# A second of every four chunks gets its right neighbour on VectorE instead of TensorE

## The chip, the cores and the metric

The kernel runs on one core of a Trainium2 chip. The metric is the device time of one execution in microseconds (us); lower is better. "DVE" in the rows is VectorE, "PE" TensorE ("PEld" its weight loads), "ACT" ScalarE, "POOL" GpSimd, "SP" the sync engine, which only issues transfers.

## What is computed

The input x is 8 images of 128 channels, 256 x 256, float32. Two layers, each of the form x + f(groupnorm(x)), follow each other. The first is the one that matters here:

```python
# each channel is shifted by its own sub-pixel amount (|theta| <= 1), so each point is a
# blend of four neighbours; then scaled per channel, then a 1x1 convolution over channels
s = z1*(1-dy)*(1-dx) + z2*(1-dy)*dx + z3*dy*(1-dx) + z4*dy*dx
s = s * w_dw[None, :, None, None]
return jnp.einsum('bchw,oc->bohw', s, w_pw)
...
x = x + _L0_conv_ref(_gn(x), L0_conv_theta_s, L0_conv_w_dw, L0_conv_w_pw)
x = x + _L1_conv_ref(_gn(x), L1_conv_w_c1, ...)
```

The second layer begins with a Haar transform and a 1x1 convolution (w_c1) on it, followed by a batch norm over all images; the rest (depthwise 3x3, two 1x1 convolutions, the way back) comes after all of that in time and isn't touched.

## The kernel before

**Three parts in time.** The first part (to about 2800 us) computes layer 0 and the first convolution of layer 1 (c1) of all images; it ends where the batch norm needs its totals. The second part (to about 3850 us) does the depthwise and 1x1 convolutions; the third writes the output. The change lies in the first part.

**Chunks, groups, images.** An image is 32 chunks of 8 rows (2048 points per channel). Four chunks are a group (`s` = 0 to 3 is the chunk's place, `SLOTS` = 4), 8 groups (`g`, `NG` = 8) are an image (`b`). Chunk number t = b * 32 + g * 4 + s. The loop over groups in the middle of an image, and the one over images 2 to 5, are hardware loops; the first and last group of an image are written out, since they carry extra work.

**What a chunk costs each engine**, in the order in which its queue has it:

- VectorE (`shift_rows`, L1311): wait for the chunk and the one below it to be in the ring; wait until TensorE has done with the buffers of two chunks ago (`conv_done`, L1322); L1333 adds the upper neighbour to the rows, giving u; two of three pieces of statistics (`count_x`, L1229) of a chunk of the next image; L1349 adds the lower neighbour to u and reports `u_done`; the third piece of statistics; L1359 adds the left neighbour, giving v. Where `three_in_v(b, s)` holds, the third piece comes behind L1359, and L1365 then adds the right neighbour to v as well, after a wait for L1359 through the counter `v_left`. `v_done` is reported by the last of them. u and v each have two buffers, for even and odd chunks.
- TensorE (`conv`, L927): four PSUM banks hold x already. Per half chunk, two matmuls of 128 x 512 float32 with `w_right` on u shifted by one column (L936; they apply the right neighbour), unless `three_in_v`; then two with `w_center` on v (L941). Then `c1`, four matmuls (L963) on a chunk of the image before. In the trace each such matmul appears as two records, so four matmuls are "x8".
- ScalarE (`shift_group`, L712): copies x into PSUM for the next chunk (`put_x`, L605), takes the result as x1 (L642), stores it (L649), squares it (L659), sums a quarter of a chunk of the next image (L673, L676), turns c1's result into y1 (L688, stored at L700) and squares it (L709).
- SP's queue (`load_image`, L377), in program order per chunk: `load_ring` loads x of a later chunk into its ring slot (L357) once `x_in_psum` and the `u_done` of a chunk three places back (four at s = 3) have been reported; `load_x1` (L375) loads a chunk of x1 of the image before back for c1, except the six that are held in SBUF; `load_x_ahead` (L346) loads a chunk of the next image for the statistics, after the counts (`x_counted`, `x_summed`) of the chunk that had the buffer. A wait in this queue holds up everything behind it.
- GpSimd copies single ring rows (L521) at the ends of a group.

The last group of an image has the moments and scales of the next image on VectorE besides (L1246 to L1275), groups 0 and 1 the padding, new weights and moments of x1 (L1239, L1278, L1292), and c1's weights (L1304, L1308) at the end of group 0. Image 7 has no next image, so no statistics; image 0 has no c1 beside it.

`three_in_v` (L314) is true for one place in four, s = 3, in images 1 to 6, for two, s = 1 and 3, in image 7 (`final(b)`), and for none in image 0.

Of the kernel before, what the change touches and what calls it, by code (L numbers as in the profile page):

```python
# [12 lines left out]
B, H, W = 8, 256, 256  # L13
# [6 lines left out]
SLOTS = 4  # L20
NG = NCH // SLOTS
# [26 lines left out]
def preact_kernel(nc, x, theta_s, w_dw, w_pwT, w_c1T, b_c1, bn1_g, bn1_b, dw_w, dw_b, gn_g, gn_b,  # L48
# [5 lines left out]
    with ExitStack() as ctx:  # L54
# [3 lines left out]
        def sem(name):  # L58
            return ctx.enter_context(nc.semaphore(name))
# [185 lines left out]
        def norm_step(s):  # L245

            return (s - NT - 2) // NT if s >= NT + 2 and (s - 2) % NT == 0 and s < TILES + NT else None
# [6 lines left out]
        def slot(s):  # L254
            return ring[:, 1 + s * ROWS:1 + (s + 1) * ROWS, :]
# [19 lines left out]
        u_up, v_done, v_left = sem("u_up"), sem("v_done"), sem("v_left")  # L275
# [25 lines left out]
        def nth(t, back=0):  # L301

            return t + (1 + LEAD - back)
# [9 lines left out]

        def three_in_v(b, s):  # L314

            return not (isinstance(b, int) and b == 0) and (s % 2 == 1 if final(b) else s == SLOTS - 1)

        def final(b):

            return isinstance(b, int) and b == B - 1  # L320
# [834 lines left out]
        def _(dve):  # L1155
# [9 lines left out]
            def done(ins):  # L1165

                steps[1] += 1
                ins.then_inc(dve_step, 1)
                dve.wait_ge(dve_step, steps[0] + steps[1])
# [51 lines left out]
            def count_x(b, g, s, pieces=range(DVE_PIECES)):  # L1221

                chunk, arrived, count = first_chunk(g, s) if isinstance(b, int) and b == 0 else \
                    (ahead[s], ahead_in[s], ahead_count(b, g))
                if 0 in pieces:
                    dve.wait_ge(arrived, count)
                i = g * SLOTS + s
                for r in pieces:
                    last = nc.vector.bn_stats(stats_x[:, bass.ds(i * (6 * DVE_PIECES) + 6 * r, 6)],  # L1229
                                              chunk[:, r * BANK:(r + 1) * BANK])  # L1230
                if DVE_PIECES - 1 in pieces:
                    last.then_inc(x_counted, 1)

            def pad_row(row):
                return ts(ring[:, row, :], ones[:, 0:1].broadcast_to([P, W]), pad_x, None, ALU.mult)

            def pad_columns(k):
                for col in (0, W + 1):
                    last = ts(u_buf[k][:, :, col], ones[:, 0:ROWS], pad_u, None, ALU.mult)  # L1239
                return last  # L1240
# [14 lines left out]
            def group_variance(n, gm, ps_means):  # L1255

                dve.wait_ge(gmom_ready, n)
                done(nc.vector.tensor_copy(gm, ps_means[:, 0:2]))
                done(stt(out=tmp, in0=gm[:, 0:1], scalar=gm[:, 0:1], in1=gm[:, 1:2],
                         op0=ALU.mult, op1=ALU.subtract))  # L1260
                done(ts(tmp, tmp, 0.0, -1.0, ALU.min, ALU.mult))
                ts(var, tmp, EPS, None, ALU.add).then_inc(var_ready, 1)
# [14 lines left out]
            def x_weights():  # L1277
                ts(w_center[:, :], pwT[:, :], scale0, None, ALU.mult)  # L1278
                ts(w_right[:, :], pwT[:, :], scale0r, None, ALU.mult).then_inc(shift_ready, 1)

            def x_bias(n):
                dve.wait_ge(vec_done, n)
                ts(bias0, ps_small_x[:, 4:5], -1.0, None, ALU.mult).then_inc(bias0_ready, 1)

            def keep_first(b):
                dve.wait_ge(sq_done, nth(b * NCH + (SLOTS - 1)))
                done(nc.vector.tensor_copy(sums_x1[:, :, 0:SLOTS], sums_first[:, :, :]))

            def x1_moments(b):
                dve.wait_ge(x1_ready, nth((b * NCH + (NCH - 1)) * 2 + 1))  # L1290
                dve.wait_ge(sq_done, nth(b * NCH + (NCH - 1)))
                nc.vector.tensor_reduce(mom[:, 0:1], sums_x1[:, 0:2, :].rearrange("p a n -> p (a n)"),  # L1292
                                        mybir.AxisListType.X, ALU.add)
                done(nc.vector.tensor_reduce(mom[:, 1:2], sums_x1[:, 2, :], mybir.AxisListType.X, ALU.add))
                ts(mom, mom, 1.0 / (H * W), None, ALU.mult).then_inc(mom_ready, 1)

            def x1_scales(n):
                group_root(n)
                tt(q1, rstd, gmom[:, 0:1], ALU.mult).then_inc(vec_ready, 1)
# [11 lines left out]
            def shift_rows(b, g, s, before, tail, ahead_of, place):  # L1311

                t = b * NCH + g * SLOTS + s
                k = s % 2
                first, last = place == "first", place == "last"
                nx, n1 = b * 2 + 2, b * 2 + 1
                for near in range(s, min(s + 2, SLOTS)):
                    dve.wait_ge(slot_in[near], b * (16 * NG) + g * 16 + 16)
                if s == 0 and not first:
                    dve.wait_ge(top_copied, b * (NG - 1) + g)  # L1320

                dve.wait_ge(conv_done, nth(t * 2 + 1, 4))  # L1322
                if first and s == 0:
                    pad_columns(0)
                    done(pad_row(0))
                if first and s == 1:
                    done(pad_columns(1))
                    if not (isinstance(b, int) and b == 0):
                        x_weights()
                if last and s == 0:  # L1330
                    done(pad_row(SLOTS * ROWS + 1))
                u = u_buf[k][:, :, 1:W + 1]
                stt(out=u, in0=ring[:, s * ROWS:(s + 1) * ROWS, :], scalar=up, in1=slot(s),  # L1333
                    op0=ALU.mult, op1=ALU.add).then_inc(u_up, 1)
                late = last and s == 0
                if first and s == 1:

                    dve.wait_ge(x1_ready, nth(b * (2 * NCH), 1))
                    x_bias(1 if isinstance(b, int) and b == 0 else b * 2)
                if first and s == 2 and before:  # L1340
                    group_variance(n1, gmom, ps_small)
                if last and s == 2 and not final(b):
                    group_variance(nx, gmom_x, ps_small_x)
                if ahead_of and not late:
                    count_x(*ahead_of, s, range(0, 2))
                dve.wait_ge(u_up, t + 1)
                if s == SLOTS - 1 and not last:
                    dve.wait_ge(bottom_copied, b * (NG - 1) + (g + 1))
                stt(out=u, in0=ring[:, s * ROWS + 2:(s + 1) * ROWS + 2, :], scalar=down, in1=u,  # L1349
                    op0=ALU.mult, op1=ALU.add).then_inc(u_done, 1)  # L1350
                if first and s == 1 and before:
                    x1_moments(b - 1)
                if late:
                    keep_first(b)
                if ahead_of and not late and not three_in_v(b, s):
                    count_x(*ahead_of, s, range(2, DVE_PIECES))
                dve.wait_ge(u_done, nth(t))
                v = v_buf[k].rearrange("p (r c) -> p r c", c=W)
                left_added = stt(out=v, in0=u_buf[k][:, :, 0:W], scalar=left, in1=u, op0=ALU.mult, op1=ALU.add)  # L1359
                if three_in_v(b, s):  # L1360
                    left_added.then_inc(v_left, 1)
                    if ahead_of and not late:
                        count_x(*ahead_of, s, range(2, DVE_PIECES))
                    dve.wait_ge(v_left, g * 2 + ((B - 2) * NG + s // 2 + 1) if final(b) else b * NG + (g + (1 - NG)))
                    stt(out=v, in0=u_buf[k][:, :, 2:W + 2], scalar=right, in1=v,  # L1365
                        op0=ALU.mult, op1=ALU.add).then_inc(v_done, 1)
                else:
                    left_added.then_inc(v_done, 1)
                if late and not final(b):
                    x_moments(b + 1, nx)  # L1370
                if ahead_of and late:
                    count_x(*ahead_of, s)
                if last and s == 2 and not final(b):
                    x_scales(nx)
                if first and s == 2 and before:
                    x1_scales(n1)
                if first and s == 3 and before:
                    c1_weights(b - 1, n1)
# [130 lines left out]
            for s in range(TILES + OLD_LAG + 2):  # L1509
                q = s - OLD_LAG  # L1510
                b = norm_step(s)
# [124 lines left out]
```

## Time and profile before

| | us |
|---|---|
| median of 3 runs | 5349.4 (5344.71 to 5351.09) |
| the profiled execution, its own time | 5349.64 |
| span in the profile | 5348.0 |
| TensorE busy | 4636.7 (87%) |
| VectorE busy | 4607.9 (86%) |
| ScalarE busy | 4341.1 (81%) |
| GpSimd busy | 1152.0 (22%) |

Rows of the trace give times from the span's start. In windows, "(x84)" is a count of instructions, PEclk the granted TensorE clock as a share of 2.4 GHz (0.5 is its lower level, 1.2 GHz), the DMA share the mean busy share of the 16 DMA engines, and GB/s what they moved. A window is attributed by start time for DMA packets. In the timeline, instructions of one line that follow each other are merged, with their count at the end.

### The profile page before, as it was taken

The numbers are of one execution on the slowest core, as the hardware profiler recorded it, in microseconds if no ns is written. First come the engines' busy times: TensorE is split into PE (matmuls) and PEld (weight loads), VectorE is DVE, ScalarE is ACT, GpSimd is POOL, SyncE is SP. The second block draws the span as 40 slices with busy tenths as digits, with TensorE's granted clock in tenths as the row PEclk, the third lists the DMA queues.
The fourth block names the chain that finished last, engine by engine and source line by source line (L and its number), as shares of the span: only waits on it lengthen the run. The fifth ranks groups of instructions, "written<-read, shape, count | busy, mean of one in ns | idle before, by whom it ended". The sixth has DMA issues, their size and how long they took to land. (4 is left out here: it accounts for less than half of the span.)

```text
span 5348.0 us, 54815 instructions
## 1 busy us (share of the span) xinstructions
PE 4636.7 (87%) x12574; PEld 2144.3 (40%) x12574; DVE 4607.9 (86%) x4207; ACT 4341.1 (81%) x6467; POOL 1152.0 (22%) x855
## 2 busy tenths in 40 slices
PE   2789999999999999999998999999987777777775
PEld 1233334344343443444443666666642222222222
DVE  7999899898998989999907999999568888888887
ACT  5788888888888888888846888888578888888887
POOL 0000000000000000000005888888301111111111
PEclk7999999999999999999999999999999999999998
DMA  8999999999999999998972333333159999999999
GB/s 337 346 351 362 426 404 414 425 383 425 394 414 425 381 425 400 416 405 332 381 283 95 134 134 135 136 136 135 51 113 225 236 236 236 236 235 236 235 236 224
DMA packets 248866, 1542.05 MB, mean 288 GB/s; under 512 B 29424, under 2 KB 29808, under 8 KB 91504
## 3 DMA queue, kind: packets, MB, share of 16 engines
q1 hardware_dynamic: 156528, 936.14, 44.9%
q0 software_dynamic: 36864, 268.45, 24.2%
q10 hardware_dynamic: 55296, 335.57, 15.0%
q8 instruction: 53, 0.87, 0.1%
q14 instruction: 125, 1.02, 0.1%
HBM read 877.35 MB, written 662.70 MB: 288 GB/s over the span
## 5 line engine op out<-in xcount | busy, mean ns | idle before, releaser
L1142 PE MATMUL ps<-arena,c2T 128*128 128x512 f32 x2048 | 1024.3, 651 | 366.8 <-ACT arena L891 364.5
L963 PE MATMUL ps<-arena 128*128 128x512 f32 x2048 | 980.8, 623 | 40.2 <-DMA arena<-out_x 23.3
L941 PE MATMUL ps<-arena 128*128 128x512 f32 x2048 | 966.0, 598 | 45.1 <-DVE arena L1365 22.4
L936 PE MATMUL ps<-arena 128*128 128x512 f32 x1536 | 740.7, 605 | 79.7 <-DVE arena L1349 35.2
L1142 PEld LDWEIGHTS ps<-arena,c2T 128*128 128x128 f32 x2048 | 401.4, 205 | 989.0 <-ACT arena L891 559.7
L891 ACT ACTIVATE arena<-ps,small 128x512 f32<-128x512 f32 x1024 | 713.7, 778 | 98.6 <-DVE arena L1574 90.1
L1333 DVE SCALAR_TENSOR_TENSOR arena<-arena,shift 128x2048 f32<-128x2048 f32 x256 | 601.8, 2351 | 162.0 <-DMA arena<-in_x 100.9
L1458 DVE SCALAR_TENSOR_TENSOR ps<-arena,taps,ps 128x256 f32<-128x256 f32 (+1 forms) x604 | 655.8, 1133 | 19.6 <-PE ps L1087 19.0
L605 ACT ACTIVATE ps<-arena 128x1024 f32<-128x1024 f32 x512 | 526.4, 1028 | 159.8 <-ACT arena L642 146.9
L521 POOL TENSOR_SCALAR arena<-arena 128x256 f32<-128x256 f32 x112 | 103.9, 936 | 2518.8 <-DMA arena<-in_x 2387.3
L642 ACT ACTIVATE arena<-ps,small 128x1024 f32<-128x1024 f32 x512 | 565.0, 1104 | 91.1 <-PE ps L941 89.3
L963 PEld LDWEIGHTS ps<-arena 128*128 128x128 f32 x2048 | 388.8, 192 | 577.7 <-issue 568.8
L941 PEld LDWEIGHTS ps<-arena 128*128 128x128 f32 x2048 | 386.6, 191 | 566.2 <-issue 469.2
L1359 DVE SCALAR_TENSOR_TENSOR arena<-arena,shift 128x2048 f32<-128x2048 f32 x256 | 599.1, 2340 | 3.5
L1349 DVE SCALAR_TENSOR_TENSOR arena<-arena,shift 128x2048 f32<-128x2048 f32 x256 | 598.6, 2338 | 1.9
L898 ACT ACTIVATE arena<-arena 128x2048 f32<-128x2048 f32 x256 | 490.4, 1916 | 113.5 <-DVE arena L1582 110.7
L1229 DVE BATCH_NORM_STATS2 arena<-arena 128x512 f32 (+1 forms) x768 | 497.2, 681 | 20.9 <-DMA arena<-in_x 20.9
L578 POOL DMA_DIRECT2D out_x<-arena x256 | 218.1, 852 | 1320.2 <-ACT arena L898 1287.2
L1581 DVE TENSOR_TENSOR arena<-arena 128x1024 f32<-128x1024 f32 x256 | 314.3, 1228 | 209.5 <-DMA out_x<-arena 208.5
L659 ACT ACTIVATE arena<-arena 128x2048 bf16<-128x2048 f32 x256 | 484.8, 1894 | 0.5 <-ACT arena L642 0.5
L936 PEld LDWEIGHTS ps<-arena 128*128 128x128 f32 x1536 | 287.1, 191 | 476.6 <-issue 350.0
L564 POOL TENSOR_TENSOR arena<-arena 128x1024 f32<-128x1024 f32 x128 | 302.9, 2367 | 99.6 <-ACT arena L840 54.5
(169 smaller groups left out, 5907.7 us busy)
## 6 DMA issues: line engine op xcount, KB each, us to landing
arena<-in_x SPq DMA_DIRECT2D x508, 1024.0 KB, 14.4
out_x<-arena ACTq DMA_DIRECT2D x256, 1024.0 KB, 9.0
out_x<-arena POOLq DMA_DIRECT2D x256, 1024.0 KB, 17.0
arena<-out_x SPq DMA_DIRECT2D x208, 1024.0 KB, 16.7
y_dram<-arena ACTq DMA_DIRECT2D x128, 512.0 KB, 8.5
arena<-y_dram SPq DMA_DIRECT2D x128, 512.0 KB, 3.6
h_dram<-arena SPq DMA_DIRECT2D x112, 512.0 KB, 2.7
arena<-h_dram SPq DMA_DIRECT2D x112, 512.0 KB, 10.2
```

The lines of the kernel that those rows point to most:

```text
L605: nc.scalar.activation(banks(half), ring[:, bass.ds(1 + s * ROWS + half * 4, 4), :] .rearrange("p r c -> p (r c)"), ACT.Copy).then_inc(x_i ...
L642: nc.scalar.activation(x1_made(s, place)[:, half * (CH // 2):(half + 1) * (CH // 2)], banks(half), ACT.Identity, bias=bias0, accum_out=tot ...
L891: last = nc.scalar.activation(g_buf[k][:, q, :], ps[:, 4 * k + q, :], ACT.Gelu, bias=z_bias[:, q:q + 1], scale=z_scale[:, q:q + 1])
L936: mm(ps[:, r, :], w_right[:, :], u_buf[k][:, 2 * r:2 * r + 2, 2:W + 2], start=False, stop=False, skip_group_check=True)
L941: last = mm(ps[:, r, :], w_center[:, :], v_buf[k][:, r * BANK:(r + 1) * BANK], start=False, stop=True, skip_group_check=True)
L963: last = mm(ps[:, 4 + s % 2, :], w_c1b[:, q, :], cells[:, q // 2, q % 2, :, :], start=(q == 0), stop=(q == 3))
L1142: last = mm(ps[:, 4 * k + q, :], c2T[:, q, :], h2[:, k * HC:(k + 1) * HC], start=True, stop=True)
L1229: last = nc.vector.bn_stats(stats_x[:, bass.ds(i * (6 * DVE_PIECES) + 6 * r, 6)], chunk[:, r * BANK:(r + 1) * BANK])
L1333: stt(out=u, in0=ring[:, s * ROWS:(s + 1) * ROWS, :], scalar=up, in1=slot(s), op0=ALU.mult, op1=ALU.add).then_inc(u_up, 1)
L1349: stt(out=u, in0=ring[:, s * ROWS + 2:(s + 1) * ROWS + 2, :], scalar=down, in1=u, op0=ALU.mult, op1=ALU.add).then_inc(u_done, 1)
L1359: left_added = stt(out=v, in0=u_buf[k][:, :, 0:W], scalar=left, in1=u, op0=ALU.mult, op1=ALU.add)
L1458: stt(out=acc, in0=h_tile(t, dy, dx, first), scalar=tap_weight(dy, dx), in1=acc, op0=ALU.mult, op1=ALU.add).then_inc(dw_acc, 1)
```

## The change

The second neighbour-in-v chunk of each group, until now only in image 7, is there in images 1 to 6 as well. In those chunks TensorE's four matmuls L936 are left out, VectorE executes L1365, and its third piece of statistics comes behind L1359 rather than before it. The value awaited on `v_left` is renumbered, since there are now two such chunks in every group from image 1 on.

```diff
@@ -313,7 +313,7 @@
         def three_in_v(b, s):
 
-            return not (isinstance(b, int) and b == 0) and (s % 2 == 1 if final(b) else s == SLOTS - 1)
+            return not (isinstance(b, int) and b == 0) and s % 2 == 1
 
@@ -1361,7 +1361,7 @@
                     left_added.then_inc(v_left, 1)
                     if ahead_of and not late:
                         count_x(*ahead_of, s, range(2, DVE_PIECES))
-                    dve.wait_ge(v_left, g * 2 + ((B - 2) * NG + s // 2 + 1) if final(b) else b * NG + (g + (1 - NG)))
+                    dve.wait_ge(v_left, b * (2 * NG) + g * 2 + (s // 2 + 1 - 2 * NG))
                     stt(out=v, in0=u_buf[k][:, :, 2:W + 2], scalar=right, in1=v,
                         op0=ALU.mult, op1=ALU.add).then_inc(v_done, 1)
```

## Rows read from the trace of the kernel before

**Rows 1.** The page, part 2: GB/s moved in 40 slices of 133.7 us.

```profile
GB/s 337 346 351 362 426 404 414 425 383 425 394 414 425 381 425 400 416 405 332 381 283 95 134 134 135 136 136 135 51 113 225 236 236 236 236 235 236 235 236 224
```

**Rows 2.** Windows, images 4 and 7: stretch, its us, busy us (count) of each engine, clock, DMA.

```profile
core 0: us, PE busy (x) PEld busy (x) DVE busy (x) ACT busy (x) POOL busy (x), PEclk, DMA share, GB/s
...
1399.70:1733.50 333.80, 317.71 (x713) 134.25 (x712) 304.38 (x246) 282.47 (x515) 12.41 (x14) 0.98 0.99 409
...
2390.00:2662.90 272.90, 270.36 (x617) 116.47 (x617) 256.47 (x131) 232.00 (x371) 21.23 (x14) 0.99 0.93 362
```

**Rows 3.** Windows, groups 0 to 7 of image 4, same columns.

```profile
1399.70:1439.90 40.20, 36.97 (x84) 15.70 (x82) 39.82 (x45) 30.84 (x57) 2.27 (x2) 0.96 0.99 402
1439.90:1481.10 41.20, 40.82 (x90) 17.68 (x91) 36.89 (x27) 33.98 (x63) 1.66 (x2) 0.96 0.84 316
1481.10:1519.50 38.40, 38.40 (x89) 16.62 (x88) 36.67 (x26) 34.01 (x64) 2.64 (x2) 1.00 1.01 425
1519.50:1559.20 39.70, 38.99 (x89) 16.46 (x88) 36.82 (x26) 34.13 (x63) 2.76 (x2) 1.00 1.01 426
1559.20:1601.60 42.40, 40.72 (x92) 16.95 (x91) 36.99 (x26) 36.84 (x69) 0.81 (x2) 1.00 1.01 424
1601.60:1644.80 43.20, 41.72 (x95) 17.50 (x94) 36.88 (x25) 37.00 (x68) 0.81 (x2) 1.00 1.01 426
1644.80:1688.80 44.00, 41.23 (x93) 16.82 (x93) 37.30 (x27) 39.02 (x70) 1.46 (x2) 1.00 1.01 425
1688.80:1733.50 44.70, 38.86 (x88) 16.52 (x87) 43.01 (x50) 36.65 (x70) 0.00 (x0) 0.96 1.01 424
```

**Rows 4.** Timeline, VectorE, image 4: start, us, instruction, [idle before <- what ended it].

```profile
1449.23 2.35 DVE L1333 SCALAR_TENSOR_TENSOR arena<-arena,shift 128x2048 f32<-128x2048 f32 x1 [0.65 <-PE ps L941]
...
1470.16 2.35 DVE L1333 SCALAR_TENSOR_TENSOR arena<-arena,shift 128x2048 f32<-128x2048 f32 x1 [1.82 <-PE ps L941]
...
1481.12 2.35 DVE L1333 SCALAR_TENSOR_TENSOR arena<-arena,shift 128x2048 f32<-128x2048 f32 x1
...
1666.44 2.35 DVE L1333 SCALAR_TENSOR_TENSOR arena<-arena,shift 128x2048 f32<-128x2048 f32 x1 [2.52 <-DMA arena<-in_x]
...
1675.01 2.35 DVE L1333 SCALAR_TENSOR_TENSOR arena<-arena,shift 128x2048 f32<-128x2048 f32 x1
```

**Rows 5.** Timeline, TensorE, group 1 and the start of group 2 of image 4.

```profile
1440.28 5.47 PE L963 MATMUL ps<-arena 128*128 128x512 f32 x8 [2.41 <-DVE small L1308]
...
1469.96 3.76 PE L963 MATMUL ps<-arena 128*128 128x512 f32 x8
...
1480.43 3.76 PE L963 MATMUL ps<-arena 128*128 128x512 f32 x8
...
1487.46 3.76 PE L963 MATMUL ps<-arena 128*128 128x512 f32 x8
```

**Rows 6.** Waits, groups 3 to 5 of image 4: total us, times, longest.

```profile
DVE arena L1333 <- DMA arena<-in_x: 9.3, 5, 2.6
```

**Rows 7.** Windows, the boundary stretches of images 1 to 7, columns as in rows 2.

```profile
401.20:482.20 81.00, 70.50 (x154) 30.25 (x153) 76.62 (x70) 61.99 (x107) 2.64 (x4) 0.94 0.88 326
688.80:812.90 124.10, 115.50 (x262) 49.59 (x261) 119.64 (x120) 101.49 (x186) 3.62 (x4) 0.97 0.97 390
1020.30:1147.20 126.90, 116.70 (x260) 49.66 (x260) 119.70 (x119) 101.58 (x187) 3.95 (x4) 0.96 0.95 380
1354.90:1481.10 126.20, 116.65 (x261) 49.91 (x260) 119.79 (x119) 101.52 (x188) 3.92 (x4) 0.96 0.95 381
1688.70:1815.90 127.20, 115.30 (x261) 49.24 (x260) 119.96 (x120) 101.82 (x188) 4.17 (x4) 0.97 0.95 378
2023.30:2147.60 124.30, 114.63 (x260) 49.21 (x259) 119.74 (x119) 102.59 (x188) 5.76 (x4) 0.97 0.97 392
2352.90:2390.00 37.10, 37.10 (x89) 16.34 (x89) 36.30 (x38) 29.04 (x51) 0.00 (x0) 1.00 0.94 364
```

**Rows 8.** DMA issues, groups 6 and 7, then group 1, of image 4: median us to landing.

```profile
arena<-in_x SPq DMA_DIRECT2D x17, 1024.0 KB, 20.2
...
arena<-in_x SPq DMA_DIRECT2D x8, 1024.0 KB, 6.0
```

## The prediction

> **What bounds the kernel now.** The change touches images 1 to 6 of the first part, so I first asked where that part is and what runs in it. The slices of the page show the DMA engines moving 425 GB/s in slice after slice up to about 2400 us, with dips to some 380 [rows 1]. Windows over whole images (from the first L1333 of one to the first of the next) give 333.8 us for image 4, of which TensorE is busy for 317.7, VectorE for 304.4, ScalarE for 282.5, and the DMA share is 0.99 [rows 2]. So four things are nearly full, and an average doesn't say which of them sets the pace. Windows by group of four chunks do [rows 3]. Groups 2 to 7 run at 424 to 426 GB/s, the same figure to within half a per cent while their lengths range from 38.4 to 44.7 us: a ceiling of the transfers, not a pace set elsewhere. Group 0 moves only 402 GB/s and group 1 only 316: there compute sets the pace. The time to landing agrees: a load of 1 MB lands 20.2 us after its issue in the stretch from group 6 on and 6.0 us in group 1 [rows 8]; loads queue in the one and not in the other.
>
> What sets groups 0 and 1 differs. In group 0 VectorE is busy 39.8 of 40.2 us and TensorE 37.0. In group 1 TensorE is busy 40.8 of 41.2 us and VectorE 36.9 [rows 3]: VectorE waits for it before L1333, 0.65 and 1.82 us in the rows shown [rows 4]. The last group is short of both: 44.7 us, VectorE busy for 43.0 (it has the moments and scales of the next image besides), DMA still at 424 GB/s [rows 3].
>
> **VectorE's added work.** A chunk with two neighbours takes 8.57 us from L1333 to L1333 (1666.44 to 1675.01), a chunk with the third addition, L1365, 10.96 (1470.16 to 1481.12) [rows 4]: 2.39 us more. The change makes s = 1 such a chunk in all 8 groups of 6 images: 48 x 2.39 = 115 us of VectorE work. A group goes from 36.8 to 39.2 us in the middle of an image.
>
> **TensorE's removed work.** The chunk loses its four L936 matmuls. From c1 block to c1 block a full chunk takes 10.47 us (1469.96 to 1480.43), one without L936 7.03 (1480.43 to 1487.46) [rows 5]: 3.44 us less, 48 x 3.44 = 165 us in all. TensorE's group falls from 3 x 10.47 + 7.03 = 38.4 us, just what group 2 takes [rows 3], to 35.0. So in compute alone the bound goes from 38.4 (TensorE) to 39.2 (VectorE).
>
> **Moved.** In chunk s = 1 the third piece of L1229 now comes behind L1359, some 2.3 us later. The look-ahead load that waits for its count is issued for the chunk four places on, and stands in SP's queue behind a ring load that waits for a later L1349 than this; I cost it at nothing. The v_left counts only number the added waits; L1365 waits for L1359 with L1229 between them, as at s = 3, and the 10.96 has that in it. Ring loads behind the later L1349 of s = 2 are issued 2.4 us later, but the chunk that reads them is later by as much. No DMA is added or removed.
>
> **Groups 2 to 6: nothing.** They take what their transfers take: image 4 needs 42.4, 43.2 and 44.0 us in groups 4 to 6 [rows 3], against 39.2 of VectorE work. VectorE waited 9.3 us on loads of x in groups 3 to 5 [rows 6]; that idle time covers the 3 x 2.39. Group 2 has the least cover: 38.4 now, 39.2 at least afterwards. It counts for nothing only because the transfers run behind, and what isn't moved in it is moved later at the same 426 GB/s. Without that queue the five groups would cost up to 12 us an image; with no excuse of any kind for waits going, 0.
>
> **Last group, group 0, group 1.** Here the transfers run dry, and what compute adds stays. The five stretches that join the last group of an image to groups 0 and 1 of the next take 124.1, 126.9, 126.2, 127.2 and 124.3 us, with VectorE busy for 119.6 to 120.0 [rows 7]. Afterwards VectorE needs 119.8 + 3 x 2.39 = 127.0. Of its waits I keep the 0.65 us in group 1 (TensorE, late from its own wait for L1308, has the same work up to that conv) and 1.0 of short waits among the small instructions (an estimate, from the 0.8 in the last row of the group [rows 7]): 128.6. The longer waits for TensorE in group 1 go: it then needs 35.0 a group. Differences: 4.5, 1.7, 2.4, 1.4, 4.3, together 14.3. The first stretch (groups 0 and 1 of image 1, 81.0 us, VectorE 76.6) becomes 76.6 + 4.8 + 1.0 = 82.4: 1.4. The last group of image 6 (37.1, VectorE 36.3) becomes 36.3 + 2.4 + 0.8 = 39.5: 2.4. Image 7 has the odd-chunk form already, and TensorE fills 270.4 of its 272.9 us [rows 2]: its work is the same, and it starts after a wait, so it gives nothing back.
>
> **Sum.** 14.3 + 1.4 + 2.4 = 18.1 us slower. Against the profiled execution's own 5349.6 us this gives 5367.7; the median of the three runs is 5349.4, so the two bases agree and I say 5367. The term I know least is the waits that go in the boundary stretches: all of them gone makes it 18.1 - 6 x 1.6 = 8 (5358), all kept at today's size (4 to 7 us a stretch) makes it 5 x 7.2 + 4.8 + 2.4 = 43 (5393).
>
> A rule weighed here: the Trainium skill (DMA: Bandwidth & Descriptors, Where 436 GB/s comes from) says that for transfers between HBM and SBUF the limit of HBM per core, about 358 GB/s, binds, and the fabric's 435 only elsewhere. The trace disagrees: 426 GB/s is held for 200 us at a time. By 358 the image's transfers alone would take 19% longer than by 426, and no edit to an engine could show; that estimate is of no use here, as the measurement decides.
>
> **Rivals.** (1) **Within 0.2%**: as above, but the boundary waits shrink nearly in full: +5 to +10 us, 5357. For it: VectorE's idle time in a boundary stretch is 4.3 to 7.2 us, and 7.2 is added. Against: group 0 has none of it.
>
> (2) **Faster**: TensorE, busy 41.7 of 43.2 us in group 5 [rows 3], is what really ends last, and 426 GB/s only follows from it. Then groups 4 to 6 fall to VectorE's 39.2, by 3.2 + 4.0 + 4.8 = 12.0, the boundary still loses about 3, and six images gain some 54: 5296. It decides from the point at which transfers can exceed 426 GB/s. Against: that rate holds equally where TensorE is full (group 2) and where it isn't (the last group, 38.9 of 44.7).
>
> (3) **Slower, waits stay**: VectorE's waits on loads remain beside the added work, because each ring load is issued only when an L1349 is done. The price is 0 to 2.39 us in each of 48 chunks, up to 115 us: 5464; half of it gives 5407. It decides where a load's time to landing doesn't shrink with the queue. Against: 20.2 us against 6.0 [rows 8] shows that it does.
>
> (4) **Slower, the clock**: with 7 us idle in each group TensorE falls to its lower level more often. After one wait of 2.41 us the c1 block took 5.47 us instead of 3.76 [rows 5], with a granted clock of 0.96 over that group [rows 3]: 1.7 us a fall. TensorE has 4.2 us to spare per group against VectorE, so one fall in each hides; where it reaches L1333 in the 18 boundary groups it adds up to 18 x 1.7 = 31: 5398. The Trainium skill (TensorE: Matmul & The Clock Gate, What's actually happening) says that throttled is the default and activity releases it, which speaks against freeing TensorE; rows 3 and 5 agree with it in kind.
>
> **How the numbers follow.** About 0.2% (11 us) is what a measurement of this kernel can tell from no change. Forecast 0.57, its own range 5358 to 5380; rival 1, 0.19; rival 2, 0.07; rival 3, 0.09; rival 4, 0.08. The forecast puts 0.05 of its chance below 5360. Faster by over 0.2%: 0.08 (rival 2 and a little noise). Within: 0.19 + 0.05 + 0.01 = 0.25. Slower: 0.67. The range leaves out rival 2 and most of 3, and takes in rival 1 and the upper bound of the waits: 5350 to 5393.
>
> **What would show it.** Right: groups 2 to 6 unchanged at 424 to 426 GB/s, with VectorE's waits before L1333 smaller by 2.4 a group; group 0 at about 42.6 us, the last group at about 46, group 1 shorter, near 39.8, with TensorE no longer full in it; L1365 x112, L936 x1152. Wrong: a rate above 430 GB/s in groups 3 to 6 (rival 2), groups 3 to 6 longer at a lower rate (rival 3), c1 blocks of over 5 us in every group with VectorE waiting for L941 (rival 4), or boundary stretches that keep their length (rival 1).

## The result, and the profile after

| | before | changed |
|---|---|---|
| median, us | 5346.99 (5344.71 to 5351.09, 9 runs) | 5362.77 (5361.2 to 5365.82, 9 runs) |
| ratio, 95% interval | | 1.0027 [1.0018, 1.0036] |
| the profiled execution's own time | 5349.64 | 5365.02 |

The change makes the kernel slower by some 16 us (10 to 19 by the interval). The profiled executions differ by 15.4.

The counts are those of the edit: TensorE's line L936 has 384 records fewer than before, that is 192 matmuls less. One row of the page, part 5 (count, busy us, mean ns, idle before):

```profile
L936 PE MATMUL ps<-arena 128*128 128x512 f32 x1152 | 567.1, 615 | 123.5 <-ACT ps L605 64.1
```

**The boundary stretches** (windows; the same seven stretches as [rows 7], from the first L1333 of the one group to the first of the other):

```profile
400.70:482.20 81.50, 67.60 (x144) 28.39 (x142) 81.05 (x72) 61.88 (x107) 5.24 (x4) 0.91 0.83 321
688.50:816.70 128.20, 110.57 (x242) 46.44 (x241) 126.42 (x123) 100.09 (x185) 4.65 (x4) 0.95 0.96 379
1024.60:1154.00 129.40, 110.86 (x240) 46.63 (x239) 126.58 (x123) 101.24 (x189) 3.72 (x4) 0.93 0.95 373
1360.70:1489.00 128.30, 110.92 (x241) 46.42 (x239) 126.41 (x122) 102.36 (x189) 4.86 (x4) 0.93 0.95 378
1698.30:1826.80 128.50, 110.82 (x242) 46.40 (x241) 126.61 (x123) 100.79 (x187) 4.68 (x4) 0.95 0.94 371
2033.80:2161.90 128.10, 109.47 (x241) 45.98 (x240) 126.39 (x123) 103.27 (x191) 5.14 (x4) 0.95 0.94 379
2367.30:2406.80 39.50, 37.21 (x84) 15.95 (x84) 38.65 (x39) 30.81 (x52) 0.00 (x0) 0.96 0.90 349
```

Together 763.5 us against 746.8 [rows 7]: 16.7 us more. VectorE is now busy for 126.4 to 126.6 us of each of the five full stretches, where it was 119.6 to 120.0: three additions more, and 2 to 3 us of idle time left where 4 to 7 had been.

**The groups of image 4** (windows, groups 0 to 7, to be laid beside [rows 3]):

```profile
1406.80:1449.30 42.50, 35.13 (x76) 14.60 (x74) 42.12 (x47) 32.31 (x59) 2.94 (x2) 0.92 0.95 378
1449.30:1489.00 39.70, 38.78 (x85) 16.47 (x85) 38.98 (x27) 31.80 (x60) 1.92 (x2) 0.96 0.89 331
1489.00:1528.10 39.10, 35.54 (x80) 14.60 (x79) 39.03 (x28) 34.68 (x65) 1.43 (x2) 1.00 1.01 423
1528.10:1567.70 39.60, 35.42 (x79) 14.33 (x78) 39.06 (x28) 34.04 (x61) 1.46 (x2) 1.00 1.01 425
1567.70:1611.50 43.80, 39.57 (x88) 15.76 (x86) 39.22 (x26) 38.24 (x71) 0.81 (x2) 1.00 1.01 426
1611.50:1654.50 43.00, 37.93 (x85) 15.39 (x84) 39.14 (x26) 36.80 (x68) 1.22 (x2) 1.00 1.01 425
1654.50:1698.30 43.80, 39.58 (x83) 16.17 (x82) 39.60 (x28) 38.32 (x68) 1.49 (x2) 0.92 1.01 426
1698.30:1744.40 46.10, 38.16 (x82) 16.02 (x81) 45.32 (x51) 37.24 (x72) 0.00 (x0) 0.92 0.98 400
```

Group 0 goes from 40.2 to 42.5 us, the last group from 44.7 to 46.1, group 1 from 41.2 to 39.7. TensorE has idle time in every group now, 35.1 busy of 42.5 in group 0; its granted clock there is 0.92 where it was 0.96. The low clock is not at the boundary alone, group 6 has 0.92 too. Groups 2 to 6 are still at 423 to 426 GB/s and take 209.3 us where they took 207.6; over all six images these groups take 1242.6 us, and took 1242.0 (sums of the distances between the first L1333 of the groups).

**In the middle of the image** VectorE's waits shrink instead of the groups growing. Waits before L1333, groups 3 to 5 of image 4; for loads it was 9.3 us in [rows 6], and for TensorE 3.2 us in the same stretch:

```profile
DVE arena L1333 <- DMA arena<-in_x: 6.8, 3, 2.7
...
DVE arena L1333 <- PE ps L941: 0.5, 1, 0.5
```

Together 12.5 us became 7.3, so 5.2 of the 7.2 us added there. Over 401 to 2390 us the same two waits fall from 149.5 to 57.7 us, by 92 of the 115 us that VectorE got to do.

DMA issues, groups 6 and 7, then group 1 (20.2 and 6.0 in [rows 8]):

```profile
arena<-in_x SPq DMA_DIRECT2D x17, 1024.0 KB, 19.4
...
arena<-in_x SPq DMA_DIRECT2D x8, 1024.0 KB, 7.3
```

**Group 1 from close by.** Timeline of VectorE, then of TensorE (start, us, instruction, idle before):

```profile
1449.26 2.34 DVE L1333 SCALAR_TENSOR_TENSOR arena<-arena,shift 128x2048 f32<-128x2048 f32 x1
...
1458.55 2.35 DVE L1333 SCALAR_TENSOR_TENSOR arena<-arena,shift 128x2048 f32<-128x2048 f32 x1 [0.65 <-PE ps L941]
...
1469.51 2.34 DVE L1333 SCALAR_TENSOR_TENSOR arena<-arena,shift 128x2048 f32<-128x2048 f32 x1
...
1478.08 2.34 DVE L1333 SCALAR_TENSOR_TENSOR arena<-arena,shift 128x2048 f32<-128x2048 f32 x1
...
1489.03 2.34 DVE L1333 SCALAR_TENSOR_TENSOR arena<-arena,shift 128x2048 f32<-128x2048 f32 x1
```

```profile
1449.60 5.48 PE L963 MATMUL ps<-arena 128*128 128x512 f32 x8 [4.30 <-DVE small L1308]
```

Chunks of 10.96 us (1458.55 to 1469.51) and of 8.57 (1469.51 to 1478.08) alternate, with the one wait of 0.65 us that was in [rows 4] too; the waits of 1.8 us are gone. TensorE waits longer for L1308 than before, 4.30 against 2.41 us [rows 5], and its c1 block takes 5.48 us, as long as before.

The slices of the page (GB/s) show the dips at the images' boundaries a little deeper, 387, 380, 390, 380 and 391 where [rows 1] has 404, 383, 394, 381 and 400, and up to 426 again between them:

```profile
GB/s 337 348 352 360 426 387 418 420 380 426 390 415 417 380 426 391 414 402 331 388 286 110 130 134 135 135 136 134 55 106 224 236 236 236 236 236 235 236 236 224
```

### The profile page after: what moved, and what is told of

It reads as the page before. It is cut to its first block and busy times, and to the rows that moved or that the text cites. A ratio compares the mean times of both kernels' runs of the same rounds, so it can differ in the third digit from the quotient of the medians.

```text
span 5363.2 us, 54145 instructions
## 1 busy us (share of the span) xinstructions
PE 4525.4 (84%) x12190; PEld 2073.6 (39%) x12190; DVE 4715.9 (88%) x4255; ACT 4341.4 (81%) x6467; POOL 1164.4 (22%) x855
## 5 line engine op out<-in xcount | busy, mean ns | idle before, releaser
L941 PE MATMUL ps<-arena 128*128 128x512 f32 x2048 | 997.2, 616 | 119.5 <-DVE arena L1365 69.4
L963 PE MATMUL ps<-arena 128*128 128x512 f32 x2048 | 974.7, 620 | 39.0 <-DVE small L1308 24.7
L1458 DVE SCALAR_TENSOR_TENSOR ps<-arena,taps,ps 128x256 f32<-128x256 f32 (+1 forms) x604 | 654.9, 1130 | 19.7 <-PE ps L1087 19.0
L936 PE MATMUL ps<-arena 128*128 128x512 f32 x1152 | 567.1, 615 | 123.5 <-ACT ps L605 64.1
L521 POOL TENSOR_SCALAR arena<-arena 128x256 f32<-128x256 f32 x112 | 116.2, 1049 | 2523.2 <-DMA arena<-in_x 2318.2
L1333 DVE SCALAR_TENSOR_TENSOR arena<-arena,shift 128x2048 f32<-128x2048 f32 x256 | 601.1, 2348 | 71.1 <-DMA arena<-in_x 49.7
L605 ACT ACTIVATE ps<-arena 128x1024 f32<-128x1024 f32 x512 | 526.3, 1028 | 159.8 <-ACT arena L642 146.9
L941 PEld LDWEIGHTS ps<-arena 128*128 128x128 f32 x2048 | 389.6, 196 | 685.6 <-issue 470.4
L963 PEld LDWEIGHTS ps<-arena 128*128 128x128 f32 x2048 | 387.7, 191 | 571.8 <-issue 560.8
L1359 DVE SCALAR_TENSOR_TENSOR arena<-arena,shift 128x2048 f32<-128x2048 f32 x256 | 599.9, 2343 | 4.9
L1229 DVE BATCH_NORM_STATS2 arena<-arena 128x512 f32 (+1 forms) x768 | 497.1, 681 | 20.2 <-DMA arena<-in_x 20.2
L936 PEld LDWEIGHTS ps<-arena 128*128 128x128 f32 x1152 | 213.6, 193 | 435.9 <-issue 255.6
```

The source lines that it names most:

```text
L605: nc.scalar.activation(banks(half), ring[:, bass.ds(1 + s * ROWS + half * 4, 4), :] .rearrange("p r c -> p (r c)"), ACT.Copy).then_inc(x_i ...
L936: mm(ps[:, r, :], w_right[:, :], u_buf[k][:, 2 * r:2 * r + 2, 2:W + 2], start=False, stop=False, skip_group_check=True)
L941: last = mm(ps[:, r, :], w_center[:, :], v_buf[k][:, r * BANK:(r + 1) * BANK], start=False, stop=True, skip_group_check=True)
L963: last = mm(ps[:, 4 + s % 2, :], w_c1b[:, q, :], cells[:, q // 2, q % 2, :, :], start=(q == 0), stop=(q == 3))
L1458: stt(out=acc, in0=h_tile(t, dy, dx, first), scalar=tap_weight(dy, dx), in1=acc, op0=ALU.mult, op1=ALU.add).then_inc(dw_acc, 1)
```

## The experiments

The first seven experiments are summed up in one table: the median and its ratio to the kernel before on the same chip, and two sums over images 1 to 6, worked out from the starts of the first addition of each group: groups 7, 0 and 1 ("ends") and groups 2 to 6 ("middle"). The sums are of the one profiled execution of each kernel, which can lie several us from its median (5349.84 against 5343.75 in the kernel with the last groups on TensorE, 5344.0 against 5350.14 in the one with the change in groups 2 to 6). The kernel before has a median of 5346.99 beside the change, 5349.58 on the chip of the experiments in groups 2 to 6, in groups 7, 0, 1 and of the two parts, and 5350.36 on the chip of the other three; each ratio is to its own.

| kernel | median us | ratio [95%] | ends us | middle us |
|---|---|---|---|---|
| before | 5346.99 | | 746.8 | 1242.0 |
| the change | 5362.77 | 1.0027 [1.0018, 1.0036] | 763.5 | 1242.6 |
| change in groups 2 to 6 | 5350.14 | 1.0002 [0.9993, 1.0011] | 745.5 | 1240.1 |
| change in groups 7, 0, 1 | 5376.01 | 1.0048 [1.0035, 1.0062] | 773.0 | 1243.0 |
| change in groups 7, 0 | 5370.01 | 1.0039 [1.0026, 1.0053] | 768.7 | 1242.3 |
| change in groups 1 to 6 | 5346.66 | 0.9992 [0.9983, 1.0001] | 743.5 | 1243.3 |
| the same, last groups on TensorE | 5343.75 | 0.9988 [0.9979, 0.9997] | 744.0 | 1242.7 |
| VectorE's part alone | 5373.79 | 1.0043 [1.003, 1.0057] | 771.8 | 1243.9 |
| TensorE's part alone | 5342.74 | 0.9988 [0.9979, 0.9997] | 742.3 | 1242.6 |

The first column to read is the last: in all nine the middle groups take 1240.1 to 1243.9 us, whatever VectorE and TensorE are given to do in them.

### The change in groups 2 to 6 only

```diff
-            return not (isinstance(b, int) and b == 0) and s % 2 == 1
+            return not (isinstance(b, int) and b == 0) and s in ((1, 3) if final(b) else IN_V[place])
...
+        IN_V = {"first": (3,), "second": (3,), "": (1, 3), "last": (3,)}
```

Group 1 is written out ahead of VectorE's loop for this, and the value awaited on `v_left` is counted accordingly; the table `IN_V` is the only thing that differs in the next ones.

> The change made in groups 2 to 6 of images 1 to 6 only (30 of its 48 chunks); groups 0, 1 and 7 as before. Theory (transfers at their ceiling set groups 2 to 6, compute sets the other three): nothing measurable, 5343 to 5352 us against 5347 before, VectorE's waits before L1333 in groups 3 to 6 smaller by about 2.4 us a group. Rival, the waits on loads stay beside the added work: 30 x 2.39 = 72 us in full, 5383 and up from half of it. Rival, TensorE ends last in the middle of an image: faster by 20 us or more.

Measured 5350.14 against 5349.58 us, ratio 1.0002 [0.9993, 1.0011]: nothing beyond some 5 us either way, as expected. Groups 2 to 6 of image 4 in one window:

```profile
1478.40:1685.70 207.30, 188.22 (x414) 76.75 (x413) 195.89 (x132) 180.63 (x328) 9.66 (x10) 0.99 1.01 426
```

207.3 us at 426 GB/s with VectorE busy for 195.9 and TensorE for 188.2; before it was 207.6 with 184.6 and 201.0. Thirty of the 48 additions are free, by that measure. The rival in which the waits stay (rival 3 of the prediction) is out.

### The change in groups 0, 1 and 7 only

```diff
-        IN_V = {"first": (3,), "second": (3,), "": (1, 3), "last": (3,)}
+        IN_V = {"first": (1, 3), "second": (1, 3), "": (3,), "last": (1, 3)}
```

> The change made in groups 0, 1 and 7 of images 1 to 6 only (18 of 48 chunks). Theory: the whole loss is here, 5361 to 5366 us (before 5347, the change 5363): group 0 at 42.5, group 1 at 39 to 40.4, the last group at 46. Rival, the loss is spread over all groups by VectorE's work: 18/48 of it, 5353.

Measured 5376.01, 26 us more than before and above the range expected: some 10 more than the theory had, so something else costs. The timeline of VectorE at the end of image 3 (L1379 is the addition of the right neighbour here, L1253 the padding that opens the next image):

```profile
1409.53 2.33 DVE L1379 SCALAR_TENSOR_TENSOR arena<-arena,shift 128x2048 f32<-128x2048 f32 x1
1415.11 0.37 DVE L1253 TENSOR_SCALAR arena<-ones,small 128x8 f32<-128x8 f32 x2 [3.24 <-PE ps L955]
```

3.24 us of idle time. The trace puts it down to TensorE, but VectorE's own sequencer has nothing on record from the branch that closes the loop over images, at 1409.13, to a register instruction at 1414.81, and only then comes to its waits; on the instruction queue two packets of 8 KB start at 1412.9 and 1413.4. It happens at the end of images 2, 3 and 4, where the loop turns, and not at the end of 1 and 5. Three times some 3.3 us are the 10 us; without them the ends are 763, as in the change. The kernel above has the same unrolled group and no such pause; its instruction queue has nothing in the last 3 us before the first addition of images 3, 4 and 5, where this one has two packets each time, and nor has that of the kernel before or of the change. That the pause is code loading is argued from these records and not shown by a run; what decides whether it occurs isn't known.

### The change in groups 0 and 7 only, loops as before

```diff
         def three_in_v(b, s, place):
...
-        IN_V = {"first": (1, 3), "second": (1, 3), "": (3,), "last": (1, 3)}
+        IN_V = {"first": (1, 3), "": (3,), "last": (1, 3)}
...
-                for s in range(SLOTS):
-                    shift_rows(b, 1, s, before, tail, (b + 1, 2) if following else None, "second")
-                with dve.Fori(2, NG - 1) as g:
+                with dve.Fori(1, NG - 1) as g:
```

> The change in groups 0 and 7 of images 1 to 6 only, with the loops as in the kernel before (no group unrolled). Theory: VectorE has no idle time there, so nearly all of 12 x 2.39 us shows, less what the last group's waits give: 5366 to 5372 us against 5347 to 5350 before; group 0 at 42.5, the last group at 46; and the turn of the image loop costs no 3.2 us, as it did in the kernel with an unrolled group. Rival, the 26 us of the ends were the addition's own and not code: 5375.

Measured 5370.01 against 5350.36, +19.7 us, without the pause. The ends are 768.7 us, 21.9 more than before: 255.1 instead of 243.8 in the six groups 0 and 270.1 instead of 259.4 in the six last groups, and nothing elsewhere.

### The change in groups 1 to 6 only

```diff
-        IN_V = {"first": (1, 3), "": (3,), "last": (1, 3)}
+        IN_V = {"first": (3,), "": (1, 3), "last": (3,)}
```

> The change in groups 1 to 6 only, loops as before. Theory: groups 2 to 6 cost nothing and group 1 gives back 1 us or so, as in the change: 5 to 6 us faster than before, 5341 to 5345 us. Rival, VectorE's work counts everywhere: slower than before by up to 36 x 2.39 = 86 us.

Measured 5346.66 against 5350.36, ratio 0.9992 [0.9983, 1.0001]: 3.7 us faster, by an interval that just touches no change, and just outside the 5341 to 5345 expected. The six groups 1 take 237.5 us instead of 243.6, but the six last groups 262.6 instead of 259.4 (45.7 us at 425 GB/s in image 3): about half of what group 1 wins comes back where the transfers are busy. With the 19.7 us of groups 0 and 7 that makes +16.0, and the change measured +15.8, closer than intervals of 5 to 7 us either way can promise. So the cost is made up of 12 chunks that lose, 6 that win a little and 30 that do nothing that can be measured.

### The same, and the last groups of images 1 to 5 wholly on TensorE

```diff
-        IN_V = {"first": (3,), "": (1, 3), "last": (3,)}
+        IN_V = {"first": (3,), "": (1, 3), "last": ()}
```

> As the one with the change in groups 1 to 6, and in the last groups of images 1 to 5 TensorE does the right neighbour of all four chunks (VectorE there 2.39 us less, 40.6; TensorE 41.9). Theory: the three groups at the boundary then need VectorE's 119.8 again instead of 122.2, and the run is 1 to 2 us an image better than the other: 5332 to 5341 us, under both kernels. Rival, the transfers, at 424 GB/s, hold the last group where it is: no gain over the other, 5341 to 5345.

Measured 5343.75, ratio 0.9988 [0.9979, 0.9997]: 0.12% faster than the kernel before, which the change is 0.27% slower than, so this version beats both; but short of the range expected, and not told apart from the kernel above. The last groups do fall, to 255.1 us from 262.6, but groups 0 rise to 250.5 from 243.4. The windows from the last group of image 3 to group 1 of image 4, of the kernel above and of this one:

```profile
1351.40:1476.50 125.10, 112.12 (x259) 47.35 (x258) 121.94 (x121) 103.55 (x191) 4.00 (x4) 1.00 0.97 387
```

```profile
1353.40:1479.40 126.00, 116.22 (x263) 49.41 (x262) 119.93 (x120) 100.37 (x185) 4.56 (x4) 0.97 0.96 378
```

VectorE has one addition less (121.9 to 119.9 busy), TensorE its 3.44 us of matmuls more (112.1 to 116.2), and neither is full. The outcome is the rival's, no gain over the other. The trace bears its reason out too, once the stretch is taken apart; 378 GB/s is the mean with groups 0 and 1 in it. The last group of image 3 and group 0 of image 4:

```profile
1353.40:1397.70 44.30, 41.09 (x94) 17.58 (x93) 40.76 (x49) 36.53 (x69) 0.00 (x0) 0.96 1.01 417
1397.70:1439.60 41.90, 36.29 (x86) 15.30 (x84) 40.09 (x46) 32.44 (x60) 2.68 (x2) 1.00 0.97 387
```

All of VectorE's longer waits in these two groups are for loads of x and none is for TensorE (timeline, VectorE; L1261 is the padding and L1355 the first addition here):

```profile
1397.04 0.37 DVE L1261 TENSOR_SCALAR arena<-ones,small 128x8 f32<-128x8 f32 x2 [1.92 <-DMA arena<-in_x]
...
1417.71 2.35 DVE L1355 SCALAR_TENSOR_TENSOR arena<-arena,shift 128x2048 f32<-128x2048 f32 x1 [1.08 <-DMA arena<-in_x]
```

They come to 4.3 us, against 1.9 in the kernel above: what VectorE is spared in the last group it then waits for loads, there and in group 0. This is read from one execution, the slowest of this kernel's eleven, and no run tests it.

### VectorE's part alone, TensorE's part alone

```diff
# VectorE's part: on the changed kernel
-                    for r in range(2 * half, 2 * half + 2) if not three_in_v(b, s) else ():
+                    for r in range(2 * half, 2 * half + 2) if not (three_in_v(b, s) and (final(b) or s == SLOTS - 1)) else ():
# TensorE's part: on the kernel before
-                    for r in range(2 * half, 2 * half + 2) if not three_in_v(b, s) else ():
+                    for r in range(2 * half, 2 * half + 2) if isinstance(b, int) and b == 0 or s % 2 == 0 else ():
```

> VectorE adds the right neighbour in chunk s = 1 of images 1 to 6, and TensorE keeps its matmuls for it there, so the neighbour is counted twice in those chunks. Theory: the loss without what TensorE gives back in group 1 (41.2 to 39.8 us and less in images 2 and 6): 5368 to 5378 us, group 1 at 41 us or over. Rival, TensorE's relief is worth nothing: 5363, as the change.

> TensorE drops the matmuls of the right neighbour in chunk s = 1 of images 1 to 6 and VectorE doesn't add it, so those chunks lack their right neighbour. Theory: only group 1 gains (VectorE's 36.9 + 0.65 against 41.2 or 39.6 us), 2 to 4 us an image, 5325 to 5335 us; groups 2 to 7 stay at 424 to 426 GB/s and at their length. Rival, TensorE ends last in the middle of an image: faster by 50 us or more, 5297 and below.

VectorE's part costs 24.2 us (5373.79), within the range; the six groups 1 take 246.6 us, against 238.4 in the change. TensorE's part gives 6.8 us (5342.74) and misses its range of 5325 to 5335: the least expected was 2 us an image, 12 in all. It was to bring group 1 to 37.5 us and brought it to between 37.5 and 40.3, and of the 8.8 us that the six groups 1 are shorter, 4.2 come back in groups 7 and 0. VectorE, then TensorE, in group 1 of image 4 with TensorE's part alone:

```profile
1447.58 2.35 DVE L1333 SCALAR_TENSOR_TENSOR arena<-arena,shift 128x2048 f32<-128x2048 f32 x1 [1.66 <-PE ps L941]
...
1458.05 2.35 DVE L1333 SCALAR_TENSOR_TENSOR arena<-arena,shift 128x2048 f32<-128x2048 f32 x1 [1.81 <-PE ps L941]
```

```profile
1437.62 6.49 PE L963 MATMUL ps<-arena 128*128 128x512 f32 x8 [4.30 <-DVE small L1308]
```

TensorE had 4.30 us of idle time before c1, and that block then took 6.49 us, where it takes 3.76 at the full clock: the wait that was to be shortened ends with a slower block, VectorE's next wait is 1.66 us (0.65 before), and the full chunk after it leaves another 1.81 (1.82 before [rows 4]). I had counted the matmuls dropped and not that the first full chunk of the group still stands in the way. Both parts leave the middle at 1242.6 and 1243.9 us, so TensorE doesn't end last there (rival 2). The parts add up to 24.2 - 6.8 = 17.4 against 15.8 for the change, well within their intervals; by the ends of the profiled executions it is 25.0 - 4.5 = 20.5 against 16.7.

### Half of the look-ahead loads

```diff
-                sp.dma_start(ahead[s], x[b, :, bass.ds((g * SLOTS + s) * CH, CH)]).then_inc(ahead_in[s], 16)
+                sp.dma_start(ahead[s][:, CH // 2:], x[b, :, bass.ds((g * SLOTS + s) * CH + CH // 2, CH // 2)]).then_inc(ahead_in[s], 16)
```

> The kernel before with only half of each look-ahead chunk loaded (the third and fourth piece; the first two pieces of statistics are taken of what the buffer still holds), so a full group moves 2.1 MB less: 15.7 MB, 36.9 us at 426 GB/s. Theory (transfers set groups 2 to 6): they fall to TensorE's 38.4 us, 6 x 5 x 38.4 = 1152 us instead of 1242, and the last groups to VectorE's 43.7: about 5255 us. Rival (426 GB/s only follows from compute): the groups keep their 41.4 us on average and the rate falls, 5347.

> The changed kernel with the same half loads. Theory: groups 2 to 6 are now VectorE's 39.1 us, 1173 us in six images, 21 more than its counterpart; with some 17 at the boundaries the change costs 38 us here, two and a half times what it costs with the full loads: about 5292 us. Rival (the transfers don't hide the addition): the same 15 us as with full loads.

| half loads | median us | ends us | middle us |
|---|---|---|---|
| before | 5298.02 | 742.1 | 1200.5 |
| the change | 5324.35 | 776.3 | 1195.4 |

Both are faster than their counterparts, 5298.02 us against 5349.49 (ratio 0.9907 [0.9891, 0.9924]), so the transfers did hold the middle groups. But both miss what was expected, 5255 and 5292 us: the change costs 26.3 us here, not 38 and not the rival's 15, the middle fell by 41 us and not by 90, and it isn't longer in the changed kernel: something else stands between the transfers and the two engines. Groups 4 and 5 of image 4, of the kernel before and of the changed one, with half loads (windows; PE, PEld, DVE, ACT and POOL busy, clock, DMA share, GB/s):

```profile
1526.70:1567.70 41.00, 39.23 (x89) 16.38 (x88) 36.93 (x26) 35.36 (x67) 2.52 (x2) 1.00 0.99 384
1567.70:1608.60 40.90, 39.31 (x89) 16.39 (x88) 36.91 (x27) 35.27 (x66) 2.52 (x2) 1.00 1.00 386
```

```profile
1544.90:1585.30 40.40, 36.12 (x81) 14.51 (x80) 39.28 (x27) 34.83 (x65) 2.52 (x2) 1.00 1.00 388
1585.30:1626.10 40.80, 36.52 (x81) 14.63 (x81) 39.17 (x27) 35.22 (x65) 2.52 (x2) 1.00 0.99 386
```

Four groups of 40.4 to 41.0 us at 384 to 388 GB/s, with TensorE at 39.3 or 36.5 and VectorE at 36.9 or 39.2. What is the same in all of them is ScalarE's 34.8 to 35.4 us of work, plus the pauses of 5 to 6 us between its instructions that groups 3 to 6 have in the kernel before and the changed one too. That is still an argument; the next pair of runs tests it. TensorE's timeline in the second names it, waiting for L605:

```profile
1557.58 1.99 PE L936 MATMUL ps<-arena 128*128 128x512 f32 x4 [1.24 <-ACT ps L605]
...
1568.48 1.98 PE L941 MATMUL ps<-arena 128*128 128x512 f32 x4 [0.18 <-ACT ps L605]
```

And at the end of an image VectorE now waits for ScalarE's sums, which it had not done (timeline, VectorE, changed kernel with half loads):

```profile
1346.32 0.22 DVE L1246 TENSOR_REDUCE part<-arena 128x2 f32<-128x64 f32 x1 [2.34 <-ACT arena L676]
```

That wait makes the last groups of images 1 to 5 48.1 to 48.8 us long there, and the 34 us of the ends are not the 17 expected.

### Half of the look-ahead loads and half of the squares

```diff
-                nc.scalar.activation(squares, x1_made(s, place), ACT.Square, accum_out=total).then_inc(sq_done, 1)
+                nc.scalar.activation(squares[:, 0:CH // 2], x1_made(s, place)[:, 0:CH // 2], ACT.Square, accum_out=total).then_inc(sq_done, 1)
```

> The kernel before with half look-ahead loads, and ScalarE squares only the first half of each x1 chunk (L659, about 0.95 us a chunk less; the sums of squares of x1 cover half the points). The pair before had groups 4 to 6 of images 2 to 5 at 40.8 to 41.1 us at 385 GB/s in both kernels. Theory formed from it: that is ScalarE's queue (35.2 us busy and 5.6 of fixed pauses). Then these groups fall to TensorE's 38.4, groups 2 to 6 of six images to about 1155 us, and the run to about 5245 to 5255. Rival, still the transfers, at a lower ceiling: nothing changes, 5298.

> The changed kernel with the same two reductions. Theory: groups 2 to 6 at VectorE's 39.1 us, 1173 us in six images, and the wait for ScalarE's sums at L1246 in the last groups (2.3 us) gone: 5285 to 5295 us, 35 to 42 us over its counterpart, since now nothing but TensorE lies under VectorE's addition. Rival, ScalarE wasn't it: 5324.

| half loads, half squares | median us | ends us | middle us |
|---|---|---|---|
| before | 5248.46 | 741.1 | 1155.3 |
| the change | 5293.86 | 763.0 | 1173.8 |

Both within the expected ranges. Groups 2 to 6 of image 4 in one window, before and changed:

```profile
1431.10:1623.70 192.60, 192.60 (x442) 83.43 (x441) 184.16 (x128) 160.11 (x321) 9.90 (x10) 1.00 1.01 405
```

```profile
1452.00:1647.60 195.60, 178.69 (x404) 75.37 (x403) 195.22 (x132) 163.69 (x328) 6.96 (x10) 1.00 1.00 400
```

TensorE is busy for all of 192.6 us in the one, 38.4 to 38.8 a group; VectorE for 195.2 of 195.6 in the other, 39.0 to 39.4 a group. Under the transfers lay ScalarE, and under ScalarE the two engines that the change weighs against each other. There it costs 45.4 us between medians (a little more than the 35 to 42 expected; 40.9 between the profiled spans).

Laid side by side, the groups of images 1 to 6 say more than their total (us, each the sum of six):

| | group 2 | group 3 | groups 4 to 6 |
|---|---|---|---|
| before | 230.6 | 239.8 | 771.6 |
| before, half loads | 230.6 | 236.5 | 733.3 |
| before, half loads, half squares | 230.6 | 230.6 | 694.1 |
| the change | 234.3 | 236.4 | 771.9 |
| the change, half loads | 234.2 | 236.1 | 725.2 |
| the change, half loads, half squares | 234.2 | 234.4 | 705.1 |

Group 2 is TensorE's already with the full loads, six times its 38.4 us, and becomes VectorE's with the change: 3.7 us longer. Group 3 takes 39.7 to 39.9 us in images 2 to 5 with the full loads, 39.9 with half of them, and falls to 38.4 only with the squares: it is ScalarE's. In image 4, with half loads and then with half squares too:

```profile
1486.80:1526.70 39.90, 38.95 (x89) 16.46 (x88) 36.94 (x26) 34.23 (x63) 2.52 (x2) 1.00 1.00 395
```

```profile
1469.50:1508.00 38.50, 38.50 (x89) 16.65 (x88) 36.78 (x27) 31.92 (x65) 1.24 (x2) 1.00 1.01 407
```

It is groups 4 to 6 that follow the loads. With the full loads the transfers set the sum of the middle groups, not the length of each: what the change loses in group 2 (3.7 us) it has back, to within 0.3 us, in group 3.

## Why the prediction was right

Forecast 5367 us, +0.33% on the profiled execution; measured 5362.77, ratio 1.0027. By its own steps:

- **VectorE's added work**, 8.57 and 10.96 us a chunk: the same in the changed trace.
- **Groups 2 to 6, nothing**: 1242.0 to 1242.6 us, and shown by itself by the change in those groups alone. The transfers are what covers it: when they are made lighter, the groups get shorter. That each of these groups takes what its transfers take is too strong: group 2 is 38.4 us whatever is loaded, and group 3 follows ScalarE's work, though both stand at 425 and 426 GB/s [rows 3]. Group 2 did become 3.7 us longer over six images, and that came back, as the prediction had said it would. VectorE's waits were to shrink by 2.4 us a group, and shrank by 1.7 in groups 3 to 5 of image 4. What the prediction also had wrong is what lies beneath. It said that in compute alone the bound goes from TensorE's 38.4 us to VectorE's 39.2, and that without the queue of transfers the five groups would cost up to 12 us an image. Beneath the transfers, at 41 us in groups 4 to 6, lies ScalarE, which it had left out of the working, and with half loads these groups cost nothing at all. With ScalarE lightened too it is 18.5 us in six images, 3.1 an image: the 12 came from taking VectorE's 2.39 us for the difference of two bounds that lie 0.6 to 0.8 apart.
- **The boundary**: predicted 82.4, five times 128.6, and 39.5; measured 81.5, 128.2, 129.4, 128.3, 128.5, 128.1 and 39.5. The sum was 18.1 us of loss against 16.7 in the trace. Group 0 was forecast at 42.6 and is at 42.5, the last group at 46 and is at 46.1, group 1 at 39.8 and is between 39.0 and 40.4.
- **TensorE's relief** counts in group 1 alone, as predicted; taken alone it gives 6.8 us, and I had put it at 12 or more before that run.
- **The gap** between forecast and result is mostly not the mechanism's: the median of nine runs before is 2.4 us below the 5349.4 of three that the sum stood on. The medians differ by 15.8 us where the sum had 18.1; of these 2.3 us, 1.4 are the boundary's (18.1 against 16.7 in the profiled executions), and the time after the last addition of the first part is 1.5 us shorter in the changed kernel's profiled execution.

The rivals: what rival 4 said of the clock did happen, and only its price didn't. The granted clock is 0.92 over groups 0, 6 and 7 of image 4, and by the clock records of the traces TensorE is at its lower level for 119.5 us of images 1 to 6, where it was for 51.2. But it has 4 to 8 us of idle time in those groups, and VectorE's waits for it have become few (waits, 401 to 2390 us):

```profile
DVE arena L1333 <- PE ps L941: 8.0, 13, 1.3
```

Before they were 48.6 us in 36 waits. So all that the clock could have cost VectorE through them is within 8.0 us, against the 31 of rival 4. Where it is seen to reach VectorE is the kernel with TensorE's part alone, in group 1. Rival 1, boundary waits shrinking in full, would have needed idle time in group 0, where there is none. Rivals 2 and 3 fell with the groups 2 to 6.

## What to carry to other kernels

When several engines and the transfers are all nearly full, moving work between two engines is paid for only in the stretches where the receiving engine ends last; here 12 of 48 additions cost all of it that can be measured. Find those stretches by windows of the loop's own period and the rate of the transfers, and put the move only where the giving engine ends last: done in groups 1 to 6 alone the same edit cost nothing, and won at most a little (3.7 us, not clear of no change). A win in one stretch can be lost again in the next, where another resource sets the pace. Before naming what lies beneath a bound, add up every engine with its fixed pauses, not only the two that the edit touches.

## What the runs showed that I had not expected

- **The DMA share doesn't say that the transfers are the bound.** It is 1.00 at 385 GB/s in the kernels with half loads, and 1.00 to 1.01 at 400 and 405 in those with half the squares too, where an engine is busy for the whole window and demonstrably sets the pace. The rate, stuck at 424 to 426 GB/s whatever the groups' length, was the better hint, but it stood there too in group 2, which was TensorE's. What decided was making the transfers lighter.
- **A turn of a loop could cost 3.2 us.** The kernel with the change in groups 7, 0 and 1 lost it at three of the loop's turns, and the trace named another engine as the cause.
- **The wait before a block doesn't say how slow the block will be.** c1 took 5.47 us after 2.41 us of idle time [rows 5], 5.48 after 4.30 in the changed kernel and 6.49 after the same 4.30 with TensorE's part alone, against 3.76 at the full clock. The difference is how much of the block ran at the lower level. Windows on TensorE within the block (us, PE busy, clock, DMA share, GB/s), of the change, then of TensorE's part alone:

```profile
1449.85:1453.26 3.41, 3.41 (x5) 0.50 1.01 382
```

```profile
1437.62:1443.20 5.58, 5.58 (x7) 0.50 1.00 410
```

At the lower level each us of work loses half a us: 3.41 / 2 and 5.58 / 2 on top of 3.76 make 5.5 and 6.6. Why the clock had fallen before the block began in the one and only after it in the other isn't settled.
